# Image tile loads issued by ScalarE's queue instead of the sync engine's, in a fused vision-tower kernel

## The chip, the cores and the metric

The kernel runs on one core of one Trainium2 chip. Such a core has a matrix engine (TensorE, PE in the profile), a vector engine (VectorE, DVE), an activation engine (ScalarE, ACT), a general engine (GpSimd, POOL) and a sync engine (SyncE, SP) that computes nothing and here issues DMAs. Each engine runs its own instruction stream in order and waits for others on semaphores. A DMA is issued by one of the engines into that engine's DMA queue, and the data is moved by 16 DMA engines that all queues share. In the profile SPq and ACTq are the issues of SP and of ACT. The metric is the device time of one execution in microseconds (us); lower is better.

## The reference

The input is 128 images of 12 channels and 224 x 224 pixels in float32. Three blocks follow one another:

```
pooled = x.reshape(Bb, Cc, n, 16, n, 16).sum(axis=(3, 5))      # 14 x 14 patches
h = einsum('bcij,ce->bije', pooled, channel_weights)           # 196 tokens of 192
h = h + attn(layernorm(h))     # 64 queries attend to the other 132 tokens,
                               # output transposed, projected; keys pass through
x2 = layernorm(h)              # then a mixture of experts:
scores = sigmoid(x2 @ gate_weight.T)       # 8 experts, best 2 groups, best 2 experts
y = sum over e of cw[t,e] * (silu(x2 @ w1[e].T) * (x2 @ w3[e].T)) @ w2[e].T
z = (silu(x2 @ sw1.T) * (x2 @ sw3.T)) @ sw2.T                  # shared expert
h = h + y + z
```

cw holds a token's router weights, zero for the experts that are not chosen. The kernel computes all eight experts for all tokens and multiplies by cw.

## The kernel before

**Groups, steps.** The images are worked on in 8 groups of 16. The expert part of a group (FFN) has 63 steps: 7 chunks of tokens times 9 experts (8 routed, one shared). Chunks 0 to 4 are keys, chunks 5 and 6 queries, whose first layer has five products a half in split float32 (L1353, against L1524 for keys). A step is pipelined over the engines: PE makes the first layer's two halves (L1524 or L1353), ACT takes silu of one (L913), POOL multiplies it by the router weights of that chunk and expert (L752), DVE multiplies by the other half (L1266), and PE makes the second layer (L1509) two steps later. The attention and router of the *next* group (its keys from step 39 on, its queries in the first steps of its own 63) are cut into some 100 items, written down by step in tables (AK_PLAN, AQ_PLAN), and each engine does its share of an item in the step named there: L1402 and L1449 are two of PE's items. Groups 1 to 4 are two passes of a loop of two groups; groups 0 and 5 to 7 are written out. By the trace the groups begin at about 200, 394, 593, 797, 1001, 1204, 1402 and 1604 us.

**Image tiles.** A group's images are 21 tiles of 128 rows by 3584 numbers (1792 KB). A tile is summed over 16 x 16 patches, its 14 columns divided between DVE (L960) and ACT (L801, one instruction pair a column), in two or three consecutive steps. The tables LATE (steps 40, 44, 46, 48, 50, 52, 53, 55, 57, 59, 61: tiles of the group after next) and EARLY (steps 1, 5, 8, ... 34: tiles of the next group) name the step at which a tile's sums begin. There are three buffers, so the load of tile t+3 needs tile t to be summed on both engines. The images of the first group and the first tiles of the next are worked on ahead of the steps, with POOL helping, at the start of the kernel.

**SP's program** (`step_dma`, `ffn_dma`): in each step it issues the router weight rows for five steps ahead (`cw_load`, L561: 128 copies of a row of the DRAM scratch cw_rows into one of 7 buffers, 192 to 256 KB), then the image load that falls due (`load`, L506), at the sixth step of a chunk the stores of the chunk before (`store`, L526), and at steps 11 and 17 the four stacking copies of the attention's output (`stack_mix`, L532, h2q<-Msb), which PE needs for L1449. LOAD_BEHIND is the number of steps between the step in which a tile's sums begin and the one in which SP issues the load into its buffer. The weight rows of a group's first steps are issued at steps 61 and 62 of the group before, behind a wait for the rows' store.

**ACT's program** (`ffn_act`): in step s it first does silu of step s+1, at the second step of a chunk evacuates output of the chunk before, then does `step_act`: the items of the step, then its columns of image tiles. ACT also issues the stores of cw_rows (L872), at the items CK and CQ.

The waits on semaphores go through one helper at L265, so part of SP's waits carry that line.

Of the kernel before, what the change touches and what calls it, by code (L numbers as in the profile page):

```python
# [39 lines left out]
NG = NB // GB  # L40
# [7 lines left out]
TILES = CG * HALF  # L48
# [7 lines left out]
STEPS = NCH * EX  # L56
# [3 lines left out]
SLOTS = 3  # L60
# [52 lines left out]
A_FIRST = 39  # L113
# [41 lines left out]
EARLY = {s: len(LATE) + i for i, s in enumerate([1, 5, 8, 12, 16, 20, 23, 27, 31, 34])}  # L155
assert len(LATE) + len(EARLY) == TILES and max(EARLY) + 2 < A_FIRST
POOL_TILES = TILES + len(LATE) - 1
LOAD_BEHIND = 3

CW_RING = 7
# [5 lines left out]
def items_at(g, step, left):  # L167

    found = [(g, kind, i) for kind, i in AQ_PLAN.get(step, [])] if g.off >= 0 else []
    if left:  # L170
        found += [(g.plus(1), kind, i) for kind, i in AK_PLAN.get(step, [])]
    return found
# [9 lines left out]
def pool_sums(g, t):  # L182

    return g.k is None and g.off * TILES + t < POOL_TILES

def tiles_at(g, step, left):

    found = []
    if left >= 1 and step in EARLY:  # L190
        found.append((g.plus(1), EARLY[step]))
    if left >= 2 and step in LATE:
        found.append((g.plus(2), LATE[step]))
    return found

def tile_parts(g, step, left, engine):

    found = []
    for back in (2, 1, 0):  # L200
        for gt_, t in tiles_at(g, step - back, left):
            parts = share(gt_, t)[engine]
            if back < len(parts):
                found.append((gt_, t, back, parts[back], back == len(parts) - 1))
    return found
# [56 lines left out]
def wait(eng, sem, value):  # L262

    if not isinstance(value, int) or value > 0:
        eng.wait_ge(sem, value)  # L265

def build(nc, x, cw, proj_w, proj_b, gate_w, gate_b, w1, w2, w3, sw1, sw2, sw3, out):
    ctx = ExitStack()
    with ctx:  # L270
        def sb(name, shape, dt=F32):
            return ctx.enter_context(nc.sbuf_tensor(name, shape, dt))

        def sem(name):
            return ctx.enter_context(nc.semaphore(name))
# [25 lines left out]
        xt = sb("xt", [128, SLOTS, ROW])  # L301
# [82 lines left out]
        x_in = [sem(f"x_in{i}") for i in range(SLOTS)]  # L384
        dve_summed, act_summed, pool_summed = sem("dve_summed"), sem("act_summed"), sem("pool_summed")
        pool_read, tree_step, rows_used = sem("pool_read"), sem("tree_step"), sem("rows_used")
# [25 lines left out]
        def x_rows(num, t):  # L412

            k, i = t // HALF, t % HALF
            return xv[num, i, 128 * k:128 * k + 128, :]
# [11 lines left out]
        P_AT = {it: i for i, it in enumerate(PREP)}  # L427

        P_DVE = [kind in ("W0", "W1", "gate") or i % 2 == 0 for i, (kind, _) in enumerate(PREP)]
        P_DVE_N = [sum(P_DVE[:i + 1]) for i in range(len(PREP))]  # L430
        P_ACT_N = [i + 1 - P_DVE_N[i] for i in range(len(PREP))]
# [40 lines left out]
        def _(sp):  # L472
# [26 lines left out]
            def load(g, t):  # L499

                for s in (dve_summed, act_summed):
                    wait(sp, s, g.at(TILES, t - SLOTS + 1))
                if pool_sums(g, t - SLOTS):
                    wait(sp, pool_read, g.at(TILES, t - SLOTS + 1))
                slot = g.slot(t)
                sp.dma_start(xt[:, slot, :], x_rows(g.num(), t)).then_inc(x_in[slot], 16)  # L506
# [28 lines left out]
            def load_after(g, t):  # L535

                if t + SLOTS < TILES:
                    load(g, t + SLOTS)
                elif g.k is not None or g.off < NG - 1:
                    load(g.plus(1), t + SLOTS - TILES)  # L540

            def cw_load(g, step):

                c, e = divmod(step, EX)
                if e == NE:
                    return
                query, col, n = CHUNKS[c]
                use = c * NE + e
                slot = use % CW_RING
                back = use - CW_RING  # L550
                if use == 0:
                    sp.wait_ge(cw_out[0], g.at(16, 16))
                elif use == NE:
                    sp.wait_ge(cw_out[1], g.at(64, 64))
                elif use == QCH * NE:
                    sp.wait_ge(cw_out[2], g.at(32, 32))
                if use in (0, NE, QCH * NE):
                    sp.sem_inc(sp_passed, 1)
                wait(sp, h_done, g.at(STEPS, back // NE * EX + back % NE + 1))
                at = col if query else 1024 + col  # L560
                sp.dma_start(cwb[slot][:, 0:n], cw_rows[g.par, e, at:at + n].partition_broadcast(128))\  # L561
                  .then_inc(cw_landed[slot], 16)

            def step_dma(g, step, left):

                if step >= 61 and left:
                    for ahead in ((0, 1) if step == 61 else (2, 3, 4)):
                        cw_load(g.plus(1), ahead)
                elif step + CW_AHEAD < STEPS and g.off >= 0:
                    cw_load(g, step + CW_AHEAD)  # L570
                if step >= LOAD_BEHIND:
                    landed = tiles_at(g, step - LOAD_BEHIND, left) if g.off >= 0 or step - LOAD_BEHIND >= A_FIRST else []
                else:
                    landed = tiles_at(g.minus(1), step - LOAD_BEHIND + STEPS, left + 1)
                for gt_, t in landed:
                    load_after(gt_, t)

            def ffn_dma(g, left, first=False):
                for step in range(STEPS):
                    if first and step == 0:  # L580

                        sp.wait_ge(rows_used, POOL_TILES)
                    step_dma(g, step, left)
                    c, e = divmod(step, EX)
                    if e == 5 and c > 0:
                        store(g, c - 1)
                    elif e == 5 and not first:
                        store(g.minus(1), NCH - 1)
                    if step in MIX:
                        stack_mix(g, MIX[step])  # L590
# [3 lines left out]
            for step in range(A_FIRST, STEPS):  # L594
                step_dma(G(None, -1), step, 2)
# [183 lines left out]
        def _(act):  # L779
# [13 lines left out]
            def act_tile(g, t, a, b, last_part=True):  # L793

                act.wait_ge(x_in[g.slot(t)], g.landed(t))
                if t == 0:
                    wait(act, aux_full, g.at(NR, R[("V", 0)] + 1 - NR))
                src = xt[:, g.slot(t), :].rearrange("p (h j w) -> p h j w", h=PATCH, j=NP)
                for j in range(a, b):
                    at = (t % HALF) * NP + j  # L800
                    last = nc.scalar.activation(src[:, :, j, :], src[:, :, j, :], ACT.Copy,  # L801
                                                accum_out=pooled[:, t // HALF, at:at + 1])
                if last_part:
                    last.then_inc(act_summed, 1)
# [77 lines left out]
            def evacuate(g, c):  # L882
# [5 lines left out]
                for b in range(2):  # L888
# [3 lines left out]
                        ins = nc.scalar.copy(st[0:64, 2 * D * b + full:2 * D * b + full + D], out_ps[b][0:64, full:full + D])  # L892
                    ins.then_inc(evac_act, 1)

            def step_act(g, step, left):

                for gi, kind, i in items_at(g, step, left):
                    item(gi, kind, i)
                for gt_, t, part, (a, b), last_part in tile_parts(g, step, left, "act"):
                    act_tile(gt_, t, a, b, last_part)  # L900
# [15 lines left out]
            def ffn_act(g, left, last=False):  # L916
                for step in range(STEPS):
                    c, e = divmod(step, EX)
                    if step + 1 < STEPS:
                        silu_act(g, step + 1)  # L920
                    elif not last:
                        silu_act(g.plus(1), 0)
                    if e == 1 and 0 < c <= QCH:
                        evacuate(g, c - 1)
                    step_act(g, step, left)

            act.wait_ge(ready, 1)
            for step in range(A_FIRST, STEPS):
                step_act(G(None, -1), step, 2)
# [653 lines left out]
```

## Time and profile before

| | |
|---|---|
| median of 3 runs | 1799.77 us (1799.73 to 1805.82) |
| profiled execution | 1794.41 us, of which span 1792.6 |
| mean granted TensorE clock | 0.950 of full speed |
| PE, DVE, ACT, POOL busy | 84%, 66%, 49%, 42% of the span |
| image loads | 168 of 1792 KB, median 8.2 us to landing |

Busy time is what an engine spends in instructions that compute; waiting and issuing are not in it. A wait in the table of waits is put down to the work that released it last. An instruction's idle time stands in square brackets behind it in the timeline, with what ended it; "issue" there means that the profile shows nothing the engine waited for. A median of landing times counts from the issue of a DMA to its completion.

### The profile page before, as it was taken

The page shows a single profiled execution, that of the slowest core. Times are in us where ns is not written, and L with a number is a line of the kernel's source. Part 1 is how long each engine was busy: PE and PEld are TensorE (multiplying, and loading weights), DVE is VectorE, ACT ScalarE, POOL GpSimd, SP SyncE. Part 2 cuts the span into 40 slices and gives each one's busy share as a digit, 9 for nine tenths or more (in the row PEclk, how much of TensorE's full clock was granted, in tenths as well). Part 3 has the DMA queues.
Part 4 walks back from the last instruction along what each step waited for, and adds up shares of the span by engine and source line. Part 5 has one row for each costly group of instructions (what it writes and reads, how often), then busy time and mean ns, then how long its engine had stood idle before and what let it go on. Part 6 is the DMA issues. An engine that isn't in the chain of part 4 may idle for free. (4 is left out here: it accounts for less than half of the span.)

```text
span 1792.6 us, 29976 instructions
## 1 busy us (share of the span) xinstructions
PE 1509.6 (84%) x9094; PEld 1184.0 (66%) x9094; DVE 1178.3 (66%) x2060; ACT 879.1 (49%) x2809; POOL 761.5 (42%) x761
## 2 busy tenths in 40 slices
PE   1721698999899988989899988999899988999997
PEld 1201575877668765877668765777668765887686
DVE  5856686687768666667768676677768666355511
ACT  2333655556545645547535655546545644335310
POOL 4327244633373234623464243633373233733431
PEclk9955799999999989999999999999999989999998
DMA  9897777778677777777777687768777775223320
GB/s 341 358 361 276 300 276 272 276 276 291 245 280 260 281 262 268 273 275 274 256 247 297 241 292 278 276 253 299 256 263 280 268 262 158 70 64 111 96 84 24
DMA packets 127672, 440.11 MB, mean 246 GB/s; under 512 B 14221, under 2 KB 80930, under 8 KB 105998
## 3 DMA queue, kind: packets, MB, share of 16 engines
q1 hardware_dynamic: 126390, 436.79, 67.6%
q10 hardware_dynamic: 1112, 1.30, 0.3%
q8 instruction: 76, 1.25, 0.3%
q14 instruction: 94, 0.77, 0.1%
HBM read 413.86 MB, written 20.07 MB: 242 GB/s over the span
## 5 line engine op out<-in xcount | busy, mean ns | idle before, releaser
L752 POOL TENSOR_TENSOR ffn<-ffn 128x384 f32<-128x384 f32 (+2 forms) x448 | 510.3, 1144 | 888.7 <-ACT ffn L913 810.2
L1509 PE MATMUL bank<-W2T,ffn 128*128 128x192 f32 (+1 forms) x3600 | 705.7, 333 | 10.2 <-ACT stage L890 5.0
L1509 PEld LDWEIGHTS bank<-W2T,ffn 128*128 128x128 f32 (+1 forms) x3600 | 604.9, 191 | 79.8 <-issue 16.5
L1266 DVE TENSOR_TENSOR ffn<-bank,ffn 128x384 f32<-128x384 f32 (+2 forms) x504 | 310.4, 617 | 349.3 <-PE bank L1353 151.8
L960 DVE TENSOR_REDUCE pooled<-xt 128x3 f32<-128x768 f32 (+2 forms) x375 | 447.8, 1195 | 18.5 <-DMA xt<-in_x 17.9
L913 ACT ACTIVATE ffn<-bank 128x384 f32<-128x384 f32 (+2 forms) x504 | 272.3, 542 | 370.3 <-PE bank L1524 141.3
L801 ACT ACTIVATE xt<-xt 128x256 f32<-128x256 f32 x809 | 329.7, 414 | 83.7 <-DMA xt<-in_x 76.1
L1524 PE MATMUL bank<-X2T,Wx 126*128 126x384 bf16 (+2 forms) x720 | 202.6, 355 | 46.7 <-DVE ffn L1266 31.9
L801 ACT ACTIVATION_READ_ACCUMULATOR xt<-xt 128x1 f32 x809 | 158.6, 196 | 0.0
L1353 PE MATMUL bank<-x0h,WT0h 128*128 128x512 f32 x288 | 130.5, 453 | 6.0 <-DVE ffn L1266 6.0
L1524 PEld LDWEIGHTS bank<-X2T,Wx 126*128 126x128 bf16 x720 | 58.2, 100 | 103.7 <-DVE ffn L1266 46.1
L1353 PE MATMUL bank<-x1l,WT1s 128*128 128x512 f32 x288 | 113.9, 395 | 0.0
L1353 PE MATMUL bank<-x1h,WT1s 128*128 128x512 f32 x288 | 113.8, 395 | 0.0
L1353 PE MATMUL bank<-x0l,WT0h 128*128 128x512 f32 x288 | 113.6, 395 | 0.0
L1353 PE MATMUL bank<-x0h,WT0l 128*128 128x512 f32 x288 | 113.6, 394 | 0.0
L707 POOL TENSOR_TENSOR stat<-stat,mhalf 98x16 f32<-98x16 f32 x32 | 94.8, 2970 | 21.9 <-DVE stat L1085 13.6
L1353 PEld LDWEIGHTS bank<-x0h,WT0h 128*128 128x128 f32 x288 | 54.3, 189 | 24.6 <-DVE ffn L1266 9.0
L1353 PEld LDWEIGHTS bank<-x1l,WT1s 128*128 128x128 f32 x288 | 54.0, 188 | 13.1
L1353 PEld LDWEIGHTS bank<-x0l,WT0h 128*128 128x128 f32 x288 | 54.0, 188 | 13.0
L1353 PEld LDWEIGHTS bank<-x1h,WT1s 128*128 128x128 f32 x288 | 54.0, 188 | 13.0
L1353 PEld LDWEIGHTS bank<-x0h,WT0l 128*128 128x128 f32 x288 | 54.4, 189 | 5.9
L841 ACT CAST UTq<-bank 126x128 bf16<-126x128 f32 x64 | 17.0, 265 | 84.0 <-PE bank L1433 84.0
(234 smaller groups left out, 1786.1 us busy)
## 6 DMA issues: line engine op xcount, KB each, us to landing
xt<-in_x SPq DMA_DIRECT2D x168, 1792.0 KB, 8.2
ffn<-cw_rows SPq DMA_DIRECT2D x192, 256.0 KB, 6.8
ffn<-cw_rows SPq DMA_DIRECT2D x192, 192.0 KB, 8.8
out<-stage SPq DMA_DIRECT2D x192, 96.0 KB
ffn<-cw_rows SPq DMA_DIRECT2D x64, 224.0 KB, 7.1
h2q<-Msb SPq DMA_DIRECT2D x64, 54.0 KB
ffn<-in_L_ffn_w SPq DMA_DIRECT2D x2, 768.0 KB
attw<-in_L_ffn_w SPq DMA_DIRECT2D x1, 512.0 KB
```

The costliest lines, as they stand in the source:

```text
L707: nc.gpsimd.tensor_tensor(out=stat[:, 3 * a + 1, u], in0=stat[:, 3 * a, u], in1=mhalf[0:HT, u], op=ALU.pow).then_inc(rstd_ready, 1)
L752: nc.gpsimd.tensor_tensor(out=cwb[slot][:, 0:n], in0=silu[(g.par + step) % 2][:, 0:n], in1=cwb[slot][:, 0:n], op=ALU.mult).then_inc(scaled, 1)
L801: last = nc.scalar.activation(src[:, :, j, :], src[:, :, j, :], ACT.Copy, accum_out=pooled[:, t // HALF, at:at + 1])
L841: nc.scalar.copy(UTq[:, :].rearrange("p (b t) -> p b t", b=GB)[:, 2 * i:2 * i + 2, :], src[:, :, 0:NQ])
L913: nc.scalar.activation(silu[(g.par + step) % 2][:, 0:n], h_ps(g, step, 0)[:, 0:n], ACT.Silu)\
L960: ins = v.tensor_reduce(out=pooled[:, t // HALF, at + lo:at + hi], in_=src[:, lo:hi, :, :], axis=AX.XY, op=ALU.add)
L1266: v.tensor_tensor(out=h[step % HR][:, 0:n], in0=h_ps(g, step, 1)[:, 0:n], in1=(silu[p] if e == NE else cwb[(c * NE + e) % CW_RING])[:, 0:n ...
L1353: ins = mm(o, left[q], right[q], start=(q == 0), stop=(q == len(left) - 1))
L1509: last = mm(o, h[step % HR][:, 128 * t:128 * t + m], W2T[:, e, :], start=(e == 0 and t % 2 == 0), stop=(e == NE), skip_group_check=True)
L1524: last = mm(o[:, 0:n], Wx[:, w:w + INTER], X2T[:, col:col + n], start=True, stop=True)
```

## The change

The image loads of the steps move from SP's program into ACT's. `step_dma` keeps them only before the first group (g.off < 0). ACT has a `load_after` of its own, which waits for the sums of the tile that held the buffer and issues the load at the start of `step_act`, ahead of the step's items and sums and behind the silu of the next step. LOAD_BEHIND goes from 3 to 4. The three buffers, the tables of steps, the weight rows, the stacking copies and the stores are unchanged. 138 image loads move; ACT's program grows from 1768 rows to 1947.

```diff
@@ -155,7 +155,7 @@
 EARLY = {s: len(LATE) + i for i, s in enumerate([1, 5, 8, 12, 16, 20, 23, 27, 31, 34])}
 assert len(LATE) + len(EARLY) == TILES and max(EARLY) + 2 < A_FIRST
 POOL_TILES = TILES + len(LATE) - 1
-LOAD_BEHIND = 3
+LOAD_BEHIND = 4
 
 
 CW_RING = 7
@@ -568,12 +568,9 @@
                         cw_load(g.plus(1), ahead)
                 elif step + CW_AHEAD < STEPS and g.off >= 0:
                     cw_load(g, step + CW_AHEAD)
-                if step >= LOAD_BEHIND:
-                    landed = tiles_at(g, step - LOAD_BEHIND, left) if g.off >= 0 or step - LOAD_BEHIND >= A_FIRST else []
-                else:
-                    landed = tiles_at(g.minus(1), step - LOAD_BEHIND + STEPS, left + 1)
-                for gt_, t in landed:
-                    load_after(gt_, t)
+                if g.off < 0 and step - LOAD_BEHIND >= A_FIRST:
+                    for gt_, t in tiles_at(g, step - LOAD_BEHIND, left):
+                        load_after(gt_, t)
 
             def ffn_dma(g, left, first=False):
                 for step in range(STEPS):
@@ -892,8 +889,25 @@
                         ins = nc.scalar.copy(st[0:64, 2 * D * b + full:2 * D * b + full + D], out_ps[b][0:64, full:full + D])
                     ins.then_inc(evac_act, 1)
 
+            def load_after(g, t):
+
+                g, t = (g, t + SLOTS) if t + SLOTS < TILES else (g.plus(1), t + SLOTS - TILES)
+                if g.k is None and g.off >= NG:
+                    return
+                wait(act, act_summed, g.at(TILES, t - SLOTS + 1))
+                wait(act, dve_summed, g.at(TILES, t - SLOTS + 1))
+                if pool_sums(g, t - SLOTS):
+                    wait(act, pool_read, g.at(TILES, t - SLOTS + 1))
+                slot = g.slot(t)
+                act.dma_start(xt[:, slot, :], x_rows(g.num(), t)).then_inc(x_in[slot], 16)
+
             def step_act(g, step, left):
 
+                if g.off >= 0:
+                    back, before, n = (g, step - LOAD_BEHIND, left) if step >= LOAD_BEHIND else \
+                        (g.minus(1), step - LOAD_BEHIND + STEPS, left + 1)
+                    for gt_, t in tiles_at(back, before, n):
+                        load_after(gt_, t)
                 for gi, kind, i in items_at(g, step, left):
                     item(gi, kind, i)
                 for gt_, t, part, (a, b), last_part in tile_parts(g, step, left, "act"):
```

SP, group 0, around step 11, before. xt<-in_x is an image load, ffn<-cw_rows weight rows, h2q<-Msb the stacking copies of step 11, out<-stage stores.

```order
L506 DMA xt<-in_x 128x3584 [waits act_summed,dve_summed]
L561 DMA ffn<-cw_rows 128x384 [waits h_done] x4
L506 DMA xt<-in_x 128x3584 [waits act_summed,dve_summed]
L561 DMA ffn<-cw_rows 128x384 [waits h_done] x3
L506 DMA xt<-in_x 128x3584 [waits act_summed,dve_summed]
L532 DMA h2q<-Msb 72x1x192 [waits aux_act]
L532 DMA h2q<-Msb 72x1x192 x3
L561 DMA ffn<-cw_rows 128x512 [waits h_done] x2
L526 DMA out<-stage 16x8x192 [waits evac_act]
L526 DMA out<-stage 16x8x192 x2
```

The same stretch of SP, changed.

```order
L561 DMA ffn<-cw_rows 128x384 [waits h_done] x7
L532 DMA h2q<-Msb 72x1x192 [waits aux_act]
L532 DMA h2q<-Msb 72x1x192 x3
L561 DMA ffn<-cw_rows 128x512 [waits h_done] x2
L526 DMA out<-stage 16x8x192 [waits evac_act]
L526 DMA out<-stage 16x8x192 x2
```

The image loads are gone from between the weight rows and ahead of the stacking copies.

SP, the last steps of group 0, up to the weight rows of group 1's first steps (the wait on cw_out_first), before.

```order
L561 DMA ffn<-cw_rows 128x512 [waits h_done] x2
L506 DMA xt<-in_x 128x3584 [waits act_summed,dve_summed]
L561 DMA ffn<-cw_rows 128x512 [waits h_done] x2
L506 DMA xt<-in_x 128x3584 [waits act_summed,dve_summed]
L561 DMA ffn<-cw_rows 128x512 [waits h_done]
L506 DMA xt<-in_x 128x3584 [waits act_summed,dve_summed] x2
L526 DMA out<-stage 2x64x192 [waits evac_dve]
L526 DMA out<-stage 2x64x192 x3
L506 DMA xt<-in_x 128x3584 [waits act_summed,dve_summed]
L561 DMA ffn<-cw_rows 128x384 [waits cw_out_first,h_done]
L561 DMA ffn<-cw_rows 128x384 [waits h_done] x4
L506 DMA xt<-in_x 128x3584 [waits act_summed,dve_summed]
```

The same stretch, changed.

```order
L561 DMA ffn<-cw_rows 128x512 [waits h_done] x6
L526 DMA out<-stage 2x64x192 [waits evac_dve]
L526 DMA out<-stage 2x64x192 x3
L561 DMA ffn<-cw_rows 128x384 [waits cw_out_first,h_done]
L561 DMA ffn<-cw_rows 128x384 [waits h_done] x4
```

Between the weight rows of the old group, the query stores and the weight rows of the new group no image load is left.

ACT, group 0, from the silu of step 57 to the items behind that of step 58, before. xt,pooled<-xt are image columns, UTq and UTk items.

```order
L913 ACTIVATE ffn<-bank 128x512 [waits scaled,h1_ready]
L841 CAST UTq<-bank 126x128 [waits aux_full]
L877 CAST UTk<-bank 126x2x16x8
L879 CAST UTk<-bank 126x8
L801 ACTIVATE xt,pooled<-xt 128x16x16 [waits x_in1]
L801 ACTIVATE xt,pooled<-xt 128x16x16
L913 ACTIVATE ffn<-bank 128x512 [waits scaled,h1_ready]
L841 CAST UTq<-bank 126x128 [waits aux_full]
L877 CAST UTk<-bank 126x2x16x8
L879 CAST UTk<-bank 126x8
```

The same stretch of ACT, changed.

```order
L927 ACTIVATE ffn<-bank 128x512 [waits scaled,h1_ready]
L902 DMA xt<-in_x 128x3584 [waits dve_summed,act_summed]
L838 CAST UTq<-bank 126x128 [waits aux_full]
L874 CAST UTk<-bank 126x2x16x8
L876 CAST UTk<-bank 126x8
L798 ACTIVATE xt,pooled<-xt 128x16x16 [waits x_in1]
L798 ACTIVATE xt,pooled<-xt 128x16x16
L927 ACTIVATE ffn<-bank 128x512 [waits scaled,h1_ready]
L902 DMA xt<-in_x 128x3584 [waits dve_summed,act_summed]
L838 CAST UTq<-bank 126x128 [waits aux_full]
L874 CAST UTk<-bank 126x2x16x8
L876 CAST UTk<-bank 126x8
```

Two image loads now stand behind the silus, ahead of the items; x_in1 and x_in2 are the semaphores on which the columns wait for a tile.

## Rows read from the trace of the kernel before

**Rows 1.** The page, busy time by engine: engine, us (share of the span), instructions.

```profile
PE 1509.6 (84%) x9094; PEld 1184.0 (66%) x9094; DVE 1178.3 (66%) x2060; ACT 879.1 (49%) x2809; POOL 761.5 (42%) x761
```

**Rows 2.** Waits of SP's queue: engine and line, releaser, us in all, times, longest us.

```profile
SPq L506 <- DVE pooled L960: 276.4, 115, 7.7
```

**Rows 3.** Waits of PE, the same columns.

```profile
PE bank L1449 <- DMA h2q<-Msb: 12.0, 7, 4.1
...
PE bank L1402 <- issue: 10.4, 5, 2.9
```

**Rows 4.** Timeline of SP, 570 to 600 us: start, length, what, [idle before <-releaser].

```profile
581.68 1.88 SPq L506 DMA_DIRECT2D xt<-in_x  x1
583.85 2.34 SPq L561 DMA_DIRECT2D ffn<-cw_rows  x5
```

**Rows 5.** Timeline of all engines, 590 to 597 us.

```profile
593.20 1.95 POOL L752 TENSOR_TENSOR ffn<-ffn 128x384 f32<-128x384 f32 x2 [8.86 <-DMA ffn<-cw_rows]
...
595.44 0.68 PE L1402 MATMUL bank<-ident,attw 64*128 64x64 f32 x8 [1.55 <-issue]
```

**Rows 6.** Timeline of PE in the last group, its L1402 and one L1449.

```profile
1605.81 0.71 PE L1402 MATMUL bank<-ident,attw 64*128 64x64 f32 x8
...
1661.51 0.26 PE L1449 MATMUL bank<-CWx,UTq 126*128 126x192 bf16 x1
```

**Rows 7.** Timeline of all engines, 832 to 847 us, first stacking of a group.

```profile
833.42 0.34 SPq L506 DMA_DIRECT2D xt<-in_x  x1
...
833.90 3.40 SPq L532 DMA_DIRECT2D h2q<-Msb  x4
...
845.36 0.26 PE L1449 MATMUL bank<-CWx,UTq 126*128 126x192 bf16 x1 [1.56 <-DMA h2q<-Msb]
```

**Rows 8.** Busy time in stretches: stretch, length, each engine (instructions), PEclk, DMA share, GB/s.

```profile
1204.00:1402.00 198.00, 179.59 (x1119) 143.46 (x1118) 142.23 (x250) 110.32 (x358) 86.89 (x74) 0.99 0.76 276
...
1003.00:1010.00 7.00, 5.73 (x38) 5.26 (x39) 4.65 (x9) 3.44 (x15) 2.10 (x3) 0.76 1.01 417
```

**Rows 9.** Timeline of all engines, 183 to 198 us, before the first group.

```profile
184.49 0.33 SPq L506 DMA_DIRECT2D xt<-in_x  x1
...
196.38 0.82 PE L1524 MATMUL bank<-X2T,Wx 126*128 126x384 bf16 x2 [4.23 <-ACT ffn L913]
```

**Rows 10.** Timeline of ACT, 1354 to 1385 us, last steps of a group.

```profile
1355.75 0.61 ACT L913 ACTIVATE ffn<-bank 128x512 f32<-128x512 f32 x1
...
1362.58 0.41 ACT L801 ACTIVATE xt<-xt 128x256 f32<-128x256 f32 x1
...
1363.78 0.58 ACT L913 ACTIVATE ffn<-bank 128x512 f32<-128x512 f32 x1
...
1370.64 0.44 ACT L801 ACTIVATE xt<-xt 128x256 f32<-128x256 f32 x1
...
1371.85 0.60 ACT L913 ACTIVATE ffn<-bank 128x512 f32<-128x512 f32 x1
...
1379.48 0.44 ACT L801 ACTIVATE xt<-xt 128x256 f32<-128x256 f32 x1
...
1380.70 0.60 ACT L913 ACTIVATE ffn<-bank 128x512 f32<-128x512 f32 x1
```

**Rows 11.** All image loads by SP's line L506.

```profile
DMA to landing us min/median/max: 6.5/8.2/15.9
```

**Rows 12.** Timeline of PE, 1354 to 1385 us.

```profile
1365.56 0.53 PE L1353 MATMUL bank<-x0h,WT0h 128*128 128x512 f32 x1
...
1374.87 0.48 PE L1353 MATMUL bank<-x0h,WT0h 128*128 128x512 f32 x1
...
1382.71 0.48 PE L1353 MATMUL bank<-x0h,WT0h 128*128 128x512 f32 x1
```

**Rows 13.** Timeline of SP, 1340 to 1404 us: the query stores of chunk 5.

```profile
1381.49 8.98 SPq L526 DMA_DIRECT2D out<-stage  x4
```

**Rows 14.** Timeline of DVE, 1354 to 1385 us: the evacuation that these stores need.

```profile
1372.66 1.01 DVE L1247 TENSOR_TENSOR stage<-bank,h2q 128x384 f32<-128x384 f32 x2
```

## Prediction

> **What bounds the kernel now.** I read the table of busy time first. TensorE (PE) is busy 1509.6 us, 84% of the span [rows 1], so a change on ACT's or SP's queue counts only through idle time of PE. The second view is the table of waits. SP, which issues nearly every DMA, waits 276.4 us in 115 pieces for DVE's sum of an image tile, at the wait that stands ahead of an image load [rows 2]; whatever comes next in SP's program stands still that long, and then lands behind a tile of 1792 KB. The same table for PE says whether anybody pays [rows 3]: 10.4 us in five pieces ahead of L1402 (one for each of five group starts) and 12.0 us in seven ahead of L1449, which waits for the stacking copies. The rest of PE's idle time per group belongs to attention and router items, which the change leaves alone.
>
> The third view is the timeline of the two places. At the start of the group at 593, SP issues an image tile from 581.68, for 1.88 us, and only then, from 583.85, the five loads of the new group's router weight rows [rows 4]. POOL's first scale then starts at 593.20, after 8.86 us of idle time, put down to those rows, and PE stands 1.55 us ahead of L1402 soon after [rows 5]. The control is the last group, when all images have been loaded: neither L1402 at its start nor its L1449 has idle time ahead [rows 6]. At a stacking, SP issues a tile at 833.42 and right behind it, on the same queue, the copies h2q<-Msb; PE stands 1.56 us until they have landed, at 845.36 [rows 7]: small copies that took eleven us because a tile was ahead.
>
> **The change part by part.** The profiled execution took 1794.4 us (span 1792.6 and 1.8 around it); the median of the runs is 1799.8, 5.4 above. I sum on the profiled one and put 5.4 on at the end.
>
> 1. *Group starts.* SP no longer waits for sums nor puts tiles ahead of the weight rows, so these go out as soon as the rows are written. The 10.4 us [rows 3] go. Bounds: 0 to 10.4. I take all of it, since the rows need only come 1.55 us earlier here [rows 5] and 2.9 at the longest [rows 3], while the tile ahead of them took 1.88 us to issue alone [rows 4] and more to move. The loop's back edge (797) has an idle time of another kind, and I take nothing for it.
>
> 2. *Stacking copies.* 12.0 us [rows 3]; bounds 0 and 12.0, taken whole, since the copies are issued in 3.40 us and wanted 8 us after that [rows 7]. What is late next at both places shows in the control: nothing that PE waits for [rows 6].
>
> 3. *Clock.* After the start at 1001 the granted clock is 0.76 of full speed over 7 us [rows 8], behind PE's idle time; 7 x 0.24 = 1.7 us. If the idle time goes, I let this go too (0 to 1.7).
>
> 4. *Before the first group* PE stands 4.23 us until 196.38, and SP issued a tile at 184.49, ahead of the first weight rows [rows 9]. In the new order that tile goes behind the first two of them. 0 to 4.2; I take 2.5.
>
> 5. *ACT issues 138 loads.* One issue took SP 0.33 us [rows 9]; 138 x 0.33 = 46 us on an engine busy half the span. Most of it lies in the time in which ACT waits for PE anyway; uncovered it costs 0.33 us where PE takes up the next silu at once. With five such loads in each of six groups that is 30 x 0.33 = 10; bounds 0 and 10, and I take 1, as the query steps have over 1 us of slack (below). The waits on sums now stand in ACT's program: behind them are the items and sums of that step and the next silu, and PE waits for that. A load goes out one step later in the program than before, four steps behind its slot's use. SP's wait lasts 276.4 / 115 = 2.4 us on average [rows 2], a step 198 / 63 = 3.1 (a group from 1204 to 1402 [rows 8]), so it is over by then and I count nothing. The longest, 7.7, would leave 4.6; one such load in each of six groups makes 27 at most.
>
> 6. *Later loads.* This is the real cost. A tile is now issued at a fixed place: behind ACT's silu of step s+5. In the last query chunks uses are dense. In the group at 1204: the load for step 53 goes out behind the silu at 1355.75 and ACT uses it at 1362.58, lead 6.6 (counted from 0.2 us into the silu; 0.4 less if the queue issues only when it has ended); that for step 55 behind 1363.78, used 1370.64, 6.7; that for step 57 behind 1371.85, used 1379.48, 7.4 [rows 10]. A tile lands after 6.5 / 8.2 / 15.9 us (least, median, most) [rows 11], so ACT will wait there. What follows a late sum is the next silu, and these have slack before PE's next layer-1 product: the silu at 1363.78 ends 1364.36 and PE starts at 1365.56, 1.2; at 1371.85, ends 1372.45, PE 1374.87, 2.4; at 1380.70, ends 1381.30, PE 1382.71, 1.4 [rows 10, 12]. With a landing time L, PE loses L-7.8, L-9.1 and L-8.8 (each if above 0). At 8.2 that is 0.4 a group. But SP, no longer held by tile sums, now sends the four query stores when DVE has evacuated them (1372.66 and 1.01 long) [rows 14], not at 1381.49 [rows 13]. They take SP 8.98 us to issue [rows 13] and now run beside the tile of step 57, issued at 1372.05, 1.6 us ahead. I take 1 us of delay for this tile: 9.2 - 8.8 = 0.4. Together 0.8 a group, six groups with loads: 5 us. Bounds: 0 (all land at 6.5), and at 15.9 for all three 22.0 a group, 132 in all; I stay near the median, since these three have an emptier queue than the median tile.
>
> Sum: -10.4 - 12.0 - 1.7 - 2.5 + 1 + 5 = -20.6; 1794.4 - 20.6 = 1773.8, and on the scale of the median **1779**.
>
> The Trainium skill, "DMA: Bandwidth & Descriptors", section "Issuing engines are not separate DMA queues", says that DMAs of the scalar, sync and gpsimd engines run on the same 16 DMA engines and interleave, and that issuing from several engines saves only the issuing time. By that alone terms 1 to 4 would be close to nothing; this is rival B. Section "Queues, rings and completion order" of the same page says that each queue has its own ring on each DMA engine and that an engine takes them in turn; by that, small transfers no longer stand behind all of a tile, and the terms hold. No row of before decides between the two: its tiles and its small loads are on one queue.
>
> **The rivals.**
>
> A, *late tiles, slower.* Place: ACT's sums at steps 53, 55 and 57. If tiles land a third of the way from median to longest, 10.8 us, PE loses 3.0 + 1.7 + 2.0 = 6.7 us in each of six groups, 40: 1794.4 - 26.6 + 1 + 40 = 1808.8, on the median's scale 1814. It outweighs the gains when the three together lose over 25.6 / 6 = 4.3 us a group, about L = 10.0. For it: tiles took up to 15.9, and the stores move onto the last of them. Against it: most long landings belong to tiles that stood behind stores and weight rows on one queue, which they now don't. 0.2.
>
> B, *shared engines, nothing gained.* The tile that was ahead on SP's queue is now beside the weight rows and copies on ACT's; on the same engines the small ones land as late as now. Gain 0, costs 6: 1794.4 + 6 = 1800.4, 1806 on the median's scale, which counts as no change. For it: with a tile on the way the DMA engines are full, a share of 1.01 behind the start at 1001 [rows 8]. Against it: in the old order the rows wait for all of a tile, and for SP's waits on sums before it, while side by side they would get a share at once. 0.12.
>
> C, *half gained.* PE's idle time goes at one of the two places, or comes back in part at the next item (a router item, the loop's back edge): -11 + 6 = -5, 1795. Also no change. 0.14.
>
> That the change doesn't do what it says is excluded by the order: no image load is left in SP's program behind the first group's start.
>
> **How the numbers follow.** Forecast 0.54, A 0.20, B 0.12, C 0.14. About 0.5% (9 us) is what a measurement of this kernel can tell from no change. The forecast's own range is 1771 (all gains, no late tile: -26.6 + 1 gives 1774, and 3 for the spread of runs) to 1790. The range that holds eight in ten has to take in B and C and the milder half of A: 1769 to 1811. Faster by over 0.5% is the forecast (0.54) and a part of C: 0.58. Slower by over 0.5% is most of A: 0.18. The rest, 0.24, is within.
>
> **What would show it.** Terms 1 and 2: ahead of L1402 and L1449 no PE idle time put down to weight rows or h2q, and POOL's first scale of a group with at most 2 us of idle time put down to a DMA. Term 3: clock near 1.0 in the 7 us after a group's start. Term 5: idle time of PE ahead of L1353 or L1524 put down to ACT hardly larger. Term 6: ACT's idle time put down to DMA xt<-in_x rises from steps 53 to 57; the tile of step 57 lands within 9.2 us. I am wrong if ACT's sums of these steps wait over 3 us each, or if weight rows still land ten us after their issue at group starts.

## Result and the profile after

| | before | changed |
|---|---|---|
| median of 12 runs | 1794.30 us | 1808.47 us (1799.99 to 1812.22) |
| profiled execution | 1794.41 us, span 1792.6 | 1808.01 us, span 1806.2 |
| PE busy | 1509.6 us | 1512.9 us |

The change made the kernel slower: ratio 1.0069, 95% interval [1.0046, 1.0092]. (The kernel before has a median of 1794.30 us over 12 runs, where the first three gave 1799.77; the 5.4 us that the prediction put on its sum were spread of runs.) Of the 13.6 us between the two spans, 10.3 are idle time of PE (span less busy time: 293.3 against 283.0) and 3.3 are time in which PE was busy longer.

The page after. The transfers now stand on two queues, q10 (ACT) and q1 (SP), in columns of packets, MB and share of 16 engines' span:

```profile
PE 1512.9 (84%) x9094; PEld 1184.7 (66%) x9094; DVE 1171.1 (65%) x2060; ACT 884.0 (49%) x2809; POOL 763.5 (42%) x761
...
q10 hardware_dynamic: 20552, 249.04, 36.6%
q1 hardware_dynamic: 106950, 189.06, 31.9%
```

PE's waits after (engine and line, releaser, us in all, times, longest). L1416 and L1463 are the L1402 and L1449 of before.

```profile
PE bank L1416 <- issue: 21.8, 3, 10.0
...
PE bank L1421 <- DVE attw L1130: 4.7, 4, 2.4
...
PE bank L1463 <- DMA h2q<-Msb: 3.1, 4, 1.2
```

The stacking copies gave back 8.9 us, as term 2 had it (12.0 to 3.1) [rows 3]. But the wait at group starts, which was to vanish, doubled (10.4 to 21.8) [rows 3], and nearly all of it lies in two of the seven starts, 9.4 and 10.0 us. One of them is the start that [rows 4, 5] show of before. SP's query stores there, before:

```profile
572.51 8.83 SPq L526 DMA_DIRECT2D out<-stage  x4
```

and SP after:

```profile
566.96 17.09 SPq L526 DMA_DIRECT2D out<-stage  x4
587.44 21.14 SPq L561 DMA_DIRECT2D ffn<-cw_rows  x10
```

POOL and PE of the same place, after:

```profile
602.55 2.91 POOL L749 TENSOR_TENSOR ffn<-ffn 128x384 f32<-128x384 f32 x3 [15.81 <-DMA ffn<-cw_rows]
...
605.61 1.08 PE L1416 MATMUL bank<-ident,attw 64*128 64x64 f32 x8 [9.41 <-issue]
```

The weight rows are issued at 587.44, after 583.85 before [rows 4], although no tile stands ahead of them on SP. What stands there is the four query stores: 17.09 us of issue. Before, the same four took 8.83 us in this group and 8.98 in another [rows 13].

The stores end at 584.05, however. From there to 587.44 SP waits for something else, the write of the weight rows into cw_rows. ACT issues this write on its own queue, where tiles now stand ahead of it: the transfer that SP waits for goes out at 581.18, 6.3 us before the first load. These waits in the whole execution (19.6 us, 2 times, before):

```profile
SPq L558 <- DMA cw_rows<-attw: 49.4, 8, 12.6
```

Of the 9.35 us by which POOL's first scale is later than before, 3.6 us are the later issue. The rest, 5.8 us, is the time to landing of the first row load, 15.0 us against 9.2; POOL's idle time ahead of that scale is 15.81 us (8.86 before) [rows 5].

The two long waits follow the two longest times of stores: ahead of these two starts the four stores took 17.09 and 18.66 us, ahead of the other four with tiles under way 12.41 to 15.72, and in the last group but one, where no tile is left to load, 4.42.

Why they take so long, the packets tell. The view of the DMA queues over 3 us in which stores are under way (packets, MB, share of 16 engines); before, 581 to 584:

```profile
q1 hardware_dynamic: 174, 0.13, 12.9%
q10 hardware_dynamic: 20, 0.02, 3.4%
```

and after, 574 to 577:

```profile
q10 hardware_dynamic: 84, 1.12, 93.0%
q1 hardware_dynamic: 8, 0.01, 0.6%
```

After the long wait the granted clock is low too (stretch, length, busy time by engine, clock, DMA share, GB/s), after:

```profile
606.00:616.00 10.00, 10.00 (x71) 8.92 (x70) 6.43 (x11) 5.33 (x21) 2.87 (x3) 0.73 0.69 241
...
1018.00:1028.00 10.00, 9.86 (x64) 8.76 (x65) 6.24 (x12) 5.18 (x20) 2.15 (x3) 0.68 0.69 243
```

In these 20 us PE is busy nearly throughout but at 0.73 and 0.68 of full speed, an estimated 5.9 us lost (10 x 0.27 + 10 x 0.32), where the prediction counted on getting 1.7 back [rows 8]. Over the whole execution PE was busy 3.3 us longer.

### The profile page after: what moved, and what is told of

Its sections match the earlier page's. It is cut to its first block and busy times, and to the rows that moved or that the text cites. A ratio compares the mean times of both kernels' runs of the same rounds, so it can differ in the third digit from the quotient of the medians.

```text
span 1806.2 us, 29976 instructions
## 1 busy us (share of the span) xinstructions
PE 1512.9 (84%) x9094; PEld 1184.7 (66%) x9094; DVE 1171.1 (65%) x2060; ACT 884.0 (49%) x2809; POOL 763.5 (42%) x761
## 3 DMA queue, kind: packets, MB, share of 16 engines
q1 hardware_dynamic: 106950, 189.06, 31.9%
## 5 line engine op out<-in xcount | busy, mean ns | idle before, releaser
L798 ACT ACTIVATE xt<-xt 128x256 f32<-128x256 f32 x809 | 329.9, 413 | 113.0 <-DMA xt<-in_x 82.1
L1538 PE MATMUL bank<-X2T,Wx 126*128 126x384 bf16 (+2 forms) x720 | 203.1, 355 | 54.8 <-DVE ffn L1280 38.9
L1538 PEld LDWEIGHTS bank<-X2T,Wx 126*128 126x128 bf16 x720 | 58.1, 99 | 111.4 <-DVE ffn L1280 52.7
L704 POOL TENSOR_TENSOR stat<-stat,mhalf 98x16 f32<-98x16 f32 x32 | 94.8, 2972 | 21.9 <-DVE stat L1099 13.6
```

Of the source, the lines that this page charges most:

```text
L704: nc.gpsimd.tensor_tensor(out=stat[:, 3 * a + 1, u], in0=stat[:, 3 * a, u], in1=mhalf[0:HT, u], op=ALU.pow).then_inc(rstd_ready, 1)
L1538: last = mm(o[:, 0:n], Wx[:, w:w + INTER], X2T[:, col:col + n], start=True, stop=True)
```

## The experiments

Theory M: the query stores, which two DMA engines carry, take turns packet by packet with the tiles of the other queue, and the weight rows wait behind them. Rivals: T, tile and weight rows hinder one another on all engines, with or without stores; A, the late image tiles of the prediction. A further rival, W, is that the rows' own write is late because it now stands behind tiles on ACT's queue, stores or not; the expectations do not name it. Ratios are to the kernel before, with 95% intervals.

**e1, query stores by image, in the changed kernel.** A store of `[2, 64, 192]` becomes two of `[64, 192]`.

```diff
...
+                if query:
+                    for j in range(n // NQ):
+                        sp.dma_start(og[col // NQ + j, 0:NQ, :],
+                                     st[NQ * (j % 2):NQ * (j % 2 + 1), j // 2, :]).then_inc(done, 16)
+                    return
                 for t in range((n + 127) // 128):
-                    if query:
-                        b0 = (col + 128 * t) // NQ
-                        dst = og[b0:b0 + 2, 0:NQ, :]
-                    else:
+                    if True:
...
```

The lines left out adapt the counts on which SP waits for the stores.

> The changed kernel, but each query store writes one image (64 rows) instead of two images (2 x 64 rows), eight DMAs for a chunk instead of four, so that its packets are spread over the DMA engines and not put on two of them. Theory M (the weight rows of a group's first steps stand behind the query stores, which two DMA engines work off one small packet in turn with a large tile packet of ACT's queue): the stores are done in a few us, the first weight rows land within 8 us of their issue, PE's idle time of 10 us at the starts of groups 2 and 4 goes, and the ratio to before falls from 1.007 to 0.982 to 0.992. Theory T (tile and weight rows alternate on all engines, stores or not): rows still land after 12 us or more, ratio 1.00 to 1.01. Theory A (late tiles in the query steps): no change, 1.005 to 1.01.

Measured 1762.58 us, ratio 0.9828 [0.9799, 0.9857]. The same stretch of SP, e1:

```profile
561.91 5.18 SPq L522 DMA_DIRECT2D out<-stage  x8
579.39 9.24 SPq L564 DMA_DIRECT2D ffn<-cw_rows  x8
```

and what POOL waits for weight rows in the whole execution, first in the changed kernel,

```profile
POOL ffn L749 <- DMA ffn<-cw_rows: 93.1, 17, 16.4
```

then in e1:

```profile
POOL ffn L752 <- DMA ffn<-cw_rows: 1.9, 1, 1.9
```

Eight stores are issued in 5.18 us where four took 17.09, and POOL's wait falls from 93.1 us to 1.9. The tiles are still on ACT's queue, beside the rows: T is out, and so is A as the main cost, since the lead of the tiles is the same and it expected 1.005 to 1.01. W is out as well: the rows' write is on ACT's queue as before, yet the first load goes out 3.2 us after it (576.14 to 579.39) and not 6.3. So the write too was late where the two-engine stores were on the way. That a store of two images keeps two engines busy is the 12.9% above. The Trainium skill, "DMA: Bandwidth & Descriptors", section "Rules for kernel authors", says that an outermost dimension of fewer than 16 confines a DMA to at most that many engines; the trace agrees (12.9% of 16 engines are 2.1).

**e2, the same stores in the kernel before.** The edit of e1, on SP's order of before.

> The kernel before with the same query stores of one image each. Theory M: the stores were ahead of tile and weight rows on SP's queue here too, 8.8 us of issue; they take about 4, and the boundary's idle time of PE (10.4 us over five groups) shrinks by half: ratio 0.992 to 0.999; the stacking copies still stand behind tiles (PE idle 12 us there stays). Theories T and A: 0.997 to 1.003.

Measured 1761.25 us, ratio 0.9823 [0.9794, 0.9853]: more than expected, and the same as e1. The wait for the copies, which was expected to stay, went too. PE's waits, e2 (L1405 and L1452 are the L1402 and L1449 of before):

```profile
PE bank L1405 <- issue: 1.7, 1, 1.7
...
PE bank L1452 <- DMA h2q<-Msb: 1.2, 3, 0.5
```

Both waits that the change was to remove [rows 3] are gone with the tiles left where they were: 10.4 to 1.7 and 12.0 to 1.2. So a tile on SP's queue does not make these waits by itself; it takes the two-engine stores on the same queue. The two waits are 19.5 of the 30.1 us by which PE's idle time fell in the profiled executions (283.0 to 252.9); the rest is in smaller pieces that were not followed up. With spread stores it makes no difference which queue issues the tiles (0.9828 and 0.9823, intervals overlapping almost wholly).

**e5, the stores of chunk 5 behind the weight rows.** In the changed kernel, SP issues them at the end of step 62.

```diff
-                    if e == 5 and c > 0:
+                    if e == 5 and 0 < c < NCH - 1:
                         store(g, c - 1)
-                    elif e == 5 and not first:
+                    elif step == STEPS - 1:
+                        store(g, NCH - 2)
+                    elif e == 5 and c == 0 and not first:
```

> The changed kernel, but SP issues the query stores of chunk 5 at the end of step 62, behind the weight rows of the next group's first steps, instead of at step 59 ahead of them; stores still on two DMA engines. Theory M: the first five weight rows land within 8 us, the 10 us idle at the starts of groups 2 and 4 go; what comes next on SP's queue (weight rows of steps 5 to 8, the stores of chunk 6) may be late instead, so ratio 0.985 to 1.000. Theory T: rows land after 12 us or more as in the changed kernel, 1.00 to 1.01. Theory A: 1.005 to 1.01.

Measured 1832.6 us, ratio 1.0217 [1.0188, 1.0245], slower than any theory had it. The time is a miss, the mechanism is not. SP in e5:

```profile
593.64 2.22 SPq L561 DMA_DIRECT2D ffn<-cw_rows  x5
596.19 19.75 SPq L526 DMA_DIRECT2D out<-stage  x4
616.06 10.35 SPq L561 DMA_DIRECT2D ffn<-cw_rows  x5
```

and POOL's scales of this group, the first and the sixth:

```profile
599.84 1.01 POOL L751 TENSOR_TENSOR ffn<-ffn 128x384 f32<-128x384 f32 x1 [3.74 <-ACT ffn L929]
...
629.27 2.90 POOL L751 TENSOR_TENSOR ffn<-ffn 128x384 f32<-128x384 f32 x3 [17.66 <-DMA ffn<-cw_rows]
```

The first scale no longer waits for its rows, though tiles are in flight on ACT's queue as in the changed kernel. But the stores now take 19.75 us, right behind the first five loads, and the rows of the next steps go out at 616.06: POOL waits 17.66 us for them, once in each of six groups, and PE up to 10.9 us with it. The wait went where the stores went.

**e4 and e6, loads a step earlier.** LOAD_BEHIND 3, in the changed kernel (e4) and on top of e1 (e6).

```diff
-LOAD_BEHIND = 4
+LOAD_BEHIND = 3
```

> The changed kernel with LOAD_BEHIND 3: ACT issues each load a step (about 3 us) earlier. Theory A: the tiles of steps 53 to 57 have 3 us more, the loss goes, ratio 0.99 to 1.00. Theory M: lead was not the limit; the tiles still alternate with the stores, ratio 1.003 to 1.012, with more idle time of ACT ahead of the load since DVE has sometimes not summed the tile yet.

> The changed kernel with one-image query stores (as e1) and with LOAD_BEHIND 3 (as e4) together. Theory A (lead of the late tiles): the step of lead still pays, so it is faster than e1 by 0.5% or more, ratio to before 0.970 to 0.978. Theory M (e4 gained only since its tiles crossed the two-engine stores less): nothing left to gain, within 0.4% of e1, 0.979 to 0.987.

Measured 1786.28 us, ratio 0.9971 [0.9950, 0.9992], and 1778.66 us, 0.9920 [0.9899, 0.9940]. Both lie outside what M expected, and e4 alone would speak for A. e6 takes that back: with the stores out of the way the earlier load does not help but costs 0.9% against e1. ACT's waits for DVE's sums in e6 and, below, in e1:

```profile
ACT xt L801 <- DVE pooled L977: 52.3, 13, 6.7
...
ACT x0h L859 <- DVE pooled L977: 25.6, 7, 3.7
```

```profile
ACT xt L801 <- DVE pooled L977: 21.3, 6, 4.0
```

Three steps behind, the load stands in ACT's program ahead of a sum that DVE has not made, and ACT stands with it; the rows name what ACT does next. In e4 this cost is there too (52.3 us on the first of these rows), and is outweighed: POOL's wait for rows, 93.1 us in the changed kernel, is there

```profile
POOL ffn L749 <- DMA ffn<-cw_rows: 40.1, 10, 6.8
```

The stores of chunk 5 take little over half the time there, 9.47 us against 17.09:

```profile
567.92 9.47 SPq L526 DMA_DIRECT2D out<-stage  x4
```

So the shift by a step moved the tiles off part of these stores; it was not lead that e4 bought.

**e7 and e8, one chunk's stores at a time.** e7 is e1 for chunk 5 only (ahead of a group's start), e8 is e2 for chunk 6 only (step 5, ahead of the stacking copies).

Against e1 and e2:

```diff
...
-                if query:
+                if query and col == 0:      # e7; e8: col == 512
                     for j in range(n // NQ):
...
```

> The changed kernel with one-image stores for chunk 5 alone (the stores at step 59, ahead of the next group's first weight rows); those of chunk 6, at step 5, stay on two DMA engines. Theory M: the first rows land about 3 us after issue and PE's idle time of 10 us at two group starts goes; the weight rows of steps 7 to 10 still stand behind chunk 6's stores, so less than e1: ratio 0.985 to 0.996. If chunk 6's stores were the main cost, 1.000 to 1.007.

> The kernel before with one-image stores for chunk 6 alone (step 5 of the next group, ahead of the stacking copies of step 11). Tiles stay on SP's queue, right ahead of those copies. If the tile ahead of the copies makes PE wait ahead of L1449 (term 2 of the prediction), the 12 us stay, ratio 0.998 to 1.002. Theory M (the two-engine stores had made tiles and copies late): they fall to 3 us or less, the 10 us at group starts stay, ratio 0.988 to 0.996.

Measured 1765.77 us, ratio 0.9846 [0.9823, 0.9869] (a little better than expected): nearly all of e1's gain over the changed kernel is the stores of chunk 5. And 1774.84 us, 0.9899 [0.9875, 0.9923]. PE's waits, e8 (L1408 and L1455 are L1402 and L1449):

```profile
PE bank L1408 <- issue: 9.0, 5, 2.8
...
PE bank L1455 <- DMA h2q<-Msb: 2.4, 3, 1.7
```

With tiles on SP's queue right ahead of the copies as before, the wait for the copies falls from 12.0 us to 2.4 while that at the starts stays (9.0). The prediction's reading of [rows 7], that the copies were late by the tile ahead of them, gives half the cause: tile and copies were both late by the stores of chunk 6, half a dozen steps earlier. Either remedy helps, since in the changed kernel the same wait fell to 3.1 us with the tile gone and the stores as they were.

**e3, only part of the loads on ACT.** SP keeps the loads behind the tiles of steps 50 to 61 and 1.

```diff
...
+SP_BEHIND = 3
+ON_SP = (50, 52, 53, 55, 57, 59, 61, 1)
...
-                    for gt_, t in tiles_at(back, before, n):
+                    for gt_, t in tiles_at(back, before, n) if before not in ON_SP else []:
...
```

> ACT issues only the loads behind the tiles of steps 5 to 48 and SP, as before and three steps behind, those behind steps 50 to 61 and 1, so the queues around a group's start are those of before; query stores on two DMA engines. Theory M: group starts as before (PE idle 10 us over five starts), stacking copies free of the tile on their queue (12 us to 3 or less): ratio 0.990 to 0.997. Theory A, late tiles of steps 53 to 57: they are loaded by SP again, so their loss goes as well, 0.990 to 0.997 with shorter waits of ACT for tiles than in the changed kernel. If the whole move of loads were the cost, in whatever step, 1.000 to 1.005.

Measured 1806.09 us, ratio 1.0071 [1.0049, 1.0092]. The copies were free as expected (1.7 us of waits ahead of them), the starts as before (10.9 us), but the time rose by 13.7 us where some 10 were to be gained: 24 us were lost elsewhere. That is outside what M and A expected (0.990 to 0.997), and nearest to the third expectation, that the whole move of loads costs something in whatever step (1.000 to 1.005). PE's rows that grew are those of L1455 and L1546 (L1433 and L1524 of before, 6.9 and 31.9 us):

```profile
PE bank L1455 <- DVE SPT L1086: 18.9, 7, 6.4
...
PE bank L1546 <- DVE ffn L1288: 41.0, 30, 3.5
```

Both wait for DVE. Timeline of e3 where the queues hand over, step 52:

```profile
1371.21 0.33 ACTq L910 DMA_DIRECT2D xt<-in_x  x1
...
1371.46 0.34 SPq L508 DMA_DIRECT2D xt<-in_x  x1
...
1380.65 0.42 ACT L806 ACTIVATE xt<-xt 128x256 f32<-128x256 f32 x1 [2.46 <-DMA xt<-in_x]
```

Two tiles are issued 0.25 us apart on two queues, and ACT waits 2.46 us for one of them. In all ACT waits 97.3 us for tiles, 76.1 before. Late tiles at the handover may be the cost here; whether they are, and for how much of the 24 us, was not isolated. M does not account for e3, and its cause stays open.

**e9 and e10, tile packets of half the size.** Each tile is loaded by two DMAs of half a row: in the changed kernel (e9) and, as control, in the kernel before (e10).

```diff
...
-                act.dma_start(xt[:, slot, :], x_rows(g.num(), t)).then_inc(x_in[slot], 16)
+                for h in (0, 1792):
+                    act.dma_start(xt[:, slot, h:h + 1792], x_rows(g.num(), t)[:, h:h + 1792]).then_inc(x_in[slot], 16)
...
```

SP's loads are split in the same way.

> The changed kernel with every image tile loaded by two DMAs of half a row each, so that tile packets are 7168 bytes and not 14336; query stores on two DMA engines as in the changed kernel. Theory M in its sharp form (on those two engines a 768-byte store packet goes out once per tile packet of ACT's queue): store packets pass about twice as often while a tile moves, the four stores of chunk 5 take 9 to 12 us to issue, not 17, and the weight rows of groups 2 and 4 land after 10 us or less, not 15; ratio 0.990 to 1.000. If the stores were slowed by something other than the turn of packets (the write itself, a shared buffer), the stores and rows stay as they are: 1.004 to 1.012.

> The control: the kernel before with tiles loaded in the same two halves, all on SP's queue, where stores and tiles stand in one order and do not take turns. Both theories: 0.995 to 1.010, the stores of chunk 5 still about 9 us; a loss would be SP's time for twice the issues and what smaller packets cost.

Measured 1782.89 us, ratio 0.9952 [0.9929, 0.9975], and for the control 1793.13 us, 0.9989 [0.9970, 1.0008]. Half the packet makes no measured difference on one queue, where the stores of chunk 5 take 8.27 us, and takes 1.2% off the changed kernel. SP in e9:

```profile
566.79 12.30 SPq L528 DMA_DIRECT2D out<-stage  x4
```

and the queues from 574 to 577 us, e9:

```profile
q10 hardware_dynamic: 116, 0.71, 60.0%
q1 hardware_dynamic: 17, 0.01, 1.2%
```

15 store packets in the 3 us against 8 (two of the 17 are of 4 bytes), and 12.30 us for the four stores against 17.09 (expected 9 to 12). The pace of the stores beside a tile follows the size of the other queue's packets: theory M in its sharp form. It does not set the whole time of the stores, which depends on how much of a tile they meet too: those of chunk 6 took 16.96 us in this group of e9 and 8.9 in the changed kernel. POOL's waits for rows in e9:

```profile
POOL ffn L751 <- DMA ffn<-cw_rows: 103.7, 37, 8.5
```

The longest is halved (16.4 to 8.5), but there are more of them, so e9 gains only a part of what e1 does.

## Why the prediction was wrong

Faster was forecast, at 1779 us; the kernel became slower, at 1808.47 us. That the range up to 1811 still held it is luck, since it was widened for other mechanisms (B, C and the milder half of A). The step that failed is in term 6 and carries term 1 with it. There the prediction saw that the query stores would now run beside a tile of the other queue, and charged this to the tile alone: "I take 1 us of delay for this tile". What was delayed was the stores, from 8.83 us to 17.09 at the start shown above and from 8.98 [rows 13] to 14.50 in the group that the prediction read, and the weight rows behind them on SP's queue. At two starts PE stood 9.4 and 10.0 us for it. The prediction's own sign of being wrong is there: at the start shown above the weight rows land 15.0 us after their issue.

1. *Group starts* (-10.4 predicted): +11.4 measured on L1416, and 4.7 more ahead of L1421, which had no such row before. That "these go out as soon as the rows are written" came true, but the write itself had moved behind tiles on ACT's queue, and the step overlooked what was left on SP's queue: once the tiles were off it, the stores were next, and two engines' turns with the tiles set when they ended and the rows behind them landed. e1, e5 and e7 show it from three sides.
2. *Stacking copies* (-12.0): -8.9, about the right size. The prediction had half the cause, as e2 and e8 show: in the changed kernel the copies came free since SP no longer carried tiles behind chunk 6's stores, and with spread stores they come free with the tile in place.
3. *Clock* (-1.7): the other way, since the idle time ahead of it grew.
4. *Before the first group* (-2.5): nothing. The rows are issued earlier but PE waits for something else. PE there, after (4.23 before) [rows 9]:

```profile
195.75 1.28 ACT L927 ACT_TABLE_LOAD   x1
...
197.59 0.82 PE L1538 MATMUL bank<-X2T,Wx 126*128 126x384 bf16 x2 [4.27 <-ACT ffn L927]
```

ACT sums its columns and loads a table, and then comes the silu that PE needs; the tile that was ahead of the rows was not the cause.

5. *ACT's issues* (+1): 135 loads stand on ACT's queue in the trace, not 138, at 0.34 us in the median. The prediction argued that four steps behind the waits for sums would be over; they were not. Its mean of 2.4 us left out what SP stood at L265 for ACT's sums, 407.4 us in 96 pieces. ACT stood once in each of six groups, within the 27 us that the prediction gave as the most:

```profile
ACT xt L798 <- DVE pooled L974: 21.8, 6, 4.0
```

A cost to PE does not show: ACT's waits for DVE ahead of its silu fell by about as much, from 46.0 to 25.6 us. e6 shows that three steps behind the waits do cost. PE's own waits for DVE ahead of L1538 rose by 7.0 us (L1524: 31.9 before), which no term had and no run isolates; in e1 they are 33.6.

```profile
PE bank L1538 <- DVE ffn L1280: 38.9, 28, 2.2
```

6. *Late tiles* (+5): ACT's waits for tiles rose by 6.0 us (76.1 to 82.1 in the tables of waits) while PE's waits for ACT's silu stayed at 11.0 us, and e6 shows that more lead gains nothing. A tile of the last query steps, after (step 53 of the group that ends at 1414; issued at 1371.10):

```profile
1371.10 0.33 ACTq L902 DMA_DIRECT2D xt<-in_x  x1
...
1378.62 0.42 ACT L798 ACTIVATE xt<-xt 128x256 f32<-128x256 f32 x1 [0.54 <-DMA xt<-in_x]
```

It landed 7.5 us after its issue and cost ACT 0.54 us, within the slack of 1.2.

Of the rivals, A had the right sign and, by chance, nearly the right time (1814): late tiles, its mechanism, are not what cost the time. B, that small transfers land as late as before on shared engines, is nearest; its 0.12 was too low and its price, no change, too mild, because it too looked at rows and tile and not at the stores between them. The Trainium skill's sentence that queues share the engines ("DMA: Bandwidth & Descriptors", section "Issuing engines are not separate DMA queues") agrees with e1 and e2: where stores are spread, the queue of the tiles makes no difference. With the two-engine stores it did, 0.7%, so by that sentence alone the result could not be had.

The best of the kernels run is the kernel before with one-image stores, at 1761.25 us, together with e1 at 1762.58; between the two no difference is measured.

## What to carry to other kernels

Before moving a large transfer to another queue, look at what stays on the old one: in this kernel small packets that only two DMA engines carry passed at their own pace while they stood on one queue with the large transfers, and took turns with their packets once they didn't. Look for DMAs that keep two of sixteen engines busy (a DMA share near 0.13 over several us) and mend those first; here that was worth 1.8%, in either order of queues. And a wait put down to a small transfer says that it was late, not what made it late: of the tile ahead of it and the stores ahead of that, only the experiment on each told what each did. Look as well at what the moved transfers now stand ahead of, here the write of the weight rows.

## What the runs showed that was not expected

- A DMA of stores can hold its issuer far longer when tiles move on the other queue: one of the four stores of a chunk took up to 10.68 us to issue in the changed kernel, 5.32 before, 0.60 in the median of both.

```profile
L526 SPq DMA_DIRECT2D out<-stage x200: 511/599/10684, 233.9 to 1797.0; - x100
```

- Beside packets of 14336 bytes 8 store packets passed in 3 us, 4 on each if two engines carry them; halving the large packet about doubled that (8 to 15).
- Idle time of 9.4 and 10.0 us of PE was followed by 10 us at a granted clock of 0.73 and 0.68, so by the estimate above the two gaps (19.4 us) cost some 5.9 us more, nearly a third of their length.
